# Stacked queries and keys brought in by groups of four pairs, each group with a semaphore of its own

## The reference

```
x = x + attention_a(layernorm(x))    # 16 heads, causal; queries and keys through low-rank products
x = x + ffn(layernorm(x))            # token shift, sigmoid gate, squared relu
x = x + attention_b(layernorm(x))    # 16 heads of 8, causal, queries and keys of length 1, scores times 8
x = x + ffn(layernorm(x))
```

## Time and profile before

| | before |
|---|---|
| three runs | 1116.02, 1116.97, 1117.32 us (median 1116.97) |
| profiled execution | 1122.54 us, of which the span of the profile is 1120.8 us |
| PE busy | 959.6 us, 86% of the span |
| DVE busy | 878.2 us, 78% |
| ACT busy | 769.6 us, 69% |
| POOL busy | 281.6 us, 25% |
| the queue of SP's transfers | 110.55 MB, 41.5% of 16 DMA engines' span |
| a batch in the steady part | 61 us (an output is stored at 523.40, 584.25, 645.10 us) |

### The profile page before, as it was taken

How to read it: one execution, slowest core, us unless ns; L and a number is a source line. 1 busy time by engine, 2 the same in 40 slices (tenths; PEclk the granted TensorE clock), 3 DMA queues, 4 the chain that set the end, 5 groups by cost and what they waited for, 6 DMA issues and landing times.

```text
span 1120.8 us, 36161 instructions
## 1 busy us (share of the span) xinstructions
PE 959.6 (86%) x15409; PEld 524.1 (47%) x15409; DVE 878.2 (78%) x2112; ACT 769.6 (69%) x1042; POOL 281.6 (25%) x264
## 2 busy tenths in 40 slices
PE   3668777979898989999999999899989999899694
PEld 1324344445454545555544545455544545455353
DVE  3757885779788898998989898989898898765632
ACT  2137464757677778777777888777877778688671
POOL 6011212212213123232323232222323232222212
PEclk8569898989998999999999999999999999899897
DMA  6155235425815427181817254362819062505130
GB/s 137 39 106 116 69 68 114 101 61 119 183 27 135 114 72 178 48 193 40 195 35 187 53 150 99 95 155 68 182 39 202 19 178 53 121 7 124 59 66 19
DMA packets 86145, 112.86 MB, mean 101 GB/s; under 512 B 13152, under 2 KB 79840, under 8 KB 79840
## 3 DMA queue, kind: packets, MB, share of 16 engines
q1 hardware_dynamic: 85984, 110.55, 41.5%
HBM read 55.22 MB, written 54.53 MB: 98 GB/s over the span
## 4 chain that ended last, share of the span: by engine, by line
PE 46%; DVE 30%; ACT 12%; issue 7%; DMA 2%; POOL 1%; SPq 0%; POOLq 0%; DVEq 0%; ACTq 0%
PE acc L722 16%; DVE rowmax L1074 12%; ACT prob L923 8%; PE pool L705 7%; PE pool L636 4%; PE pool L749 3%; PE pool L755 3%; DVE xn L1032 2%; PE pool L777 2%; PE pool L601 2%; PE pool L652 2%; DVE stats L1020 2%; PE pool L763 2%; PE pool L674 2%; DVE rest_k L1045 2%
## 5 line engine op out<-in xcount | busy, mean ns | idle before, releaser
L923 ACT ACTIVATE prob<-pool 128x1024 f32<-128x1024 f32 x576 | 565.5, 1029 | 150.5 <-PE pool L652 146.1
L1074 DVE TENSOR_REDUCE rowmax<-pool 128x2 f32<-128x1024 f32 (+7 forms) x480 | 357.8, 792 | 92.9 <-PE pool L652 89.9
L722 PE MATMUL acc<-prob,vals_a 128*32 128x512 f32 (+7 forms) x2048 | 169.3, 426 | 0.2 <-ACT prob L923 0.2
L722 PE MATMUL acc<-prob,vals_b 128*32 128x512 f32 (+7 forms) x2048 | 166.4, 426 | 1.2 <-DVE turned_b L1109 0.7
L636 PE MATMUL pool<-stack_ka,stack_qa 48*64 48x512 bf16 (+7 forms) x2048 | 118.7, 305 | 47.3 <-issue 13.9
L705 PE MATMUL pool<-stack_qa,stack_ka 51*64 51x512 bf16 (+7 forms) x2048 | 113.7, 302 | 31.3 <-DVE rowmax L1074 18.2
L705 PE MATMUL pool<-stack_qb,stack_kb 48*64 48x512 bf16 (+7 forms) x2048 | 113.7, 298 | 23.4 <-ACT prob L923 9.7
L652 PE MATMUL pool<-mask_t,ident_b 64*64 64x128 bf16 (+1 forms) x2304 | 130.7, 216 | 1.8 <-issue 1.8
L636 PEld LDWEIGHTS pool<-stack_ka,stack_qa 48*64 48x64 bf16 x2048 | 42.8, 109 | 141.0 <-ACT prob L923 59.3
L1284 POOL TENSOR_TENSOR rstd<-mv,minus_half 128x4 f32<-128x4 f32 x64 | 65.4, 1021 | 153.1 <-DVE mv L1027 153.1
L1296 POOL TENSOR_TENSOR parts_q<-rest_q,parts_q 128x512 bf16<-128x512 f32 x32 | 37.1, 1158 | 186.7 <-DVE parts_q L1048 186.6
(11 more groups left out here) (129 smaller groups left out, 1386.6 us busy)
## 6 DMA issues: line engine op xcount, KB each, us to landing
stack_qa<-scratch_qa SPq DMA_DIRECT2D x32, 384.0 KB, 7.9
stack_ka<-scratch_ka SPq DMA_DIRECT2D x32, 384.0 KB, 7.8
stack_kb<-scratch_kb SPq DMA_DIRECT2D x32, 384.0 KB, 5.6
stack_qb<-scratch_qb SPq DMA_DIRECT2D x32, 384.0 KB, 6.9
scratch_qa<-parts_q SPq DMA_DIRECT2D x16, 384.0 KB, 3.6
scratch_ka<-parts_k SPq DMA_DIRECT2D x16, 384.0 KB, 6.2
scratch_qb<-parts_q SPq DMA_DIRECT2D x16, 384.0 KB, 2.6
scratch_kb<-parts_k SPq DMA_DIRECT2D x16, 384.0 KB, 2.6
```

What stands on the lines that cost most here:

```text
L722: last = eng.matmul(acc[32 * j:32 * j + 32, BLK * blk:T], vals[a][:, blk, GROUP * g + j, :], prob[n % NPROB][:, k, at:at + T - BLK * blk], ...
L923: eng.activation(prob[n % NPROB][:, :, :], place["unit", n][0][:, :, :], ACT.Exp, scale=scale).then_inc(S["exped"], 1)
L1074: last = eng.tensor_reduce(to, of, axis=AX.X, op=ALU.max)
```

## The change

`restack` now takes a group instead of a tensor. In its first slot it brings group 0 of both tensors, and in its second slot group 1 of both; the order of the tensors in a slot is q, k for attention a and k, q for attention b. Each of its transfers is half as large (48 rows of 2048 elements in place of 4096), and there are twice as many: 256 instead of 128 in the whole program. Each group of each stack has a semaphore of its own. `row_maxima` and `attend` wait for their own group's alone, and SP waits, ahead of a group, only until that group's former contents are scored. The writes to scratch wait for both groups of the batch before.

```diff
-            for what in ("projected_", "part0_", "rest_", "part1_", "part2_", "written_", "stacked_"):
+            for what in ("stacked_" + n + str(g) for g in range(GROUPS)):
+                S[what] = ctx.enter_context(nc.semaphore("s_" + what))
+            for what in ("projected_", "part0_", "rest_", "part1_", "part2_", "written_"):
...
-            for k, n in enumerate("qk"):
-                yield e.restack(b, n, "a"), [max(at("restack_a")[k], front[-1] + 1, end_a[2] + k)]
+            for k in range(GROUPS):
+                yield e.restack(b, k, "a"), [max(at("restack_a")[k], front[-1] + 1, end_a[2] + k)]
...
-            for k, n in enumerate("kq"):
-                yield e.restack(b, n, "b"), [max(at("restack_b")[k], back[-1] + 1, of_b - 2 * SLOTS + k)]
+            for k in range(GROUPS):
+                yield e.restack(b, k, "b"), [max(at("restack_b")[k], back[-1] + 1, of_b - 2 * SLOTS + k)]
...
             def row_maxima(self, b, g, units):
                 eng, q = self.eng, self.q
-                q.wait_ge(S["stacked_qa"], 32 * (b + 1))
-                q.wait_ge(S["stacked_ka"], 32 * (b + 1))
+                q.wait_ge(S[f"stacked_qa{g}"], 32 * (b + 1))
+                q.wait_ge(S[f"stacked_ka{g}"], 32 * (b + 1))
...
-                        q.wait_ge(S[f"stacked_q{a}"], 32 * (b + 1))
-                        q.wait_ge(S[f"stacked_k{a}"], 32 * (b + 1))
+                        q.wait_ge(S[f"stacked_q{a}{g}"], 32 * (b + 1))
+                        q.wait_ge(S[f"stacked_k{a}{g}"], 32 * (b + 1))
...
-                    q.wait_ge(S[f"stacked_{n}{a}"], 32 * b)
+
+                    for g in range(GROUPS):
+                        q.wait_ge(S[f"stacked_{n}{a}{g}"], 32 * b)
...
-            def restack(self, b, n, a):
-                eng, q = self.eng, self.q
-                to = stack[n + a][b % len(stack[n + a])]
-                if n + a == "ka":
-                    q.wait_ge(S["ones_rows"], min(2 * b + 2, 4))
-
-                b_ = b - len(stack[n + a])
-                if b_ >= 0:
-                    q.wait_ge(S["scored"], unit_of[a, b_][-1] + 1)
-                q.wait_ge(S[f"written_{n}{a}"], 48 * (b + 1))
-                for r in range(2):
-                    src = scratch[n + a].rearrange("t (d r a) c -> (t d) r (a c)", d=D, r=2)[:, r, :]
-                    eng.dma_start(to[BLK * r:BLK * r + ROWS, :, :].rearrange("p a c -> p (a c)"),
-                                  src).then_inc(S[f"stacked_{n}{a}"], 16)
+            def restack(self, b, g, a):
+                eng, q = self.eng, self.q
+
+                for n in "qk" if a == "a" else "kq":
+                    to = stack[n + a][b % len(stack[n + a])]
+                    if n + a == "ka":
+                        q.wait_ge(S["ones_rows"], min(2 * b + 2, 4))
+
+                    b_ = b - len(stack[n + a])
+                    if b_ >= 0:
+                        q.wait_ge(S["scored"], unit_of[a, b_][9 * g + 8] + 1)
+                    q.wait_ge(S[f"written_{n}{a}"], 48 * (b + 1))
+                    for r in range(2):
+                        src = scratch[n + a].rearrange("t (d r a) c -> (t d) r a c", d=D, r=2)
+                        eng.dma_start(to[BLK * r:BLK * r + ROWS, GROUP * g:GROUP * g + GROUP, :],
+                                      src[:, r, GROUP * g:GROUP * g + GROUP, :]).then_inc(S[f"stacked_{n}{a}{g}"], 16)
```

## The result

| | before | after |
|---|---|---|
| median (runs of one chip) | 1116.49 us (1113.40 to 1117.32) | 1098.00 us (1094.58 to 1098.68) |
| ratio | | 0.9833, interval 0.9805 to 0.9862 |
| profiled execution, span | 1122.54 us, 1120.8 us | 1098.68 us, 1096.9 us |

The change makes the kernel 18.5 us faster. A second set of runs on another chip gave 1097.69 us beside 1116.0 (0.9843, 0.9812 to 0.9873).

The account below looks back on a forecast made before the run. PE and DVE were taken to alternate, with PE waiting for stacks only in batches 0 and 1; 4.9 + 4.8 + 1.0 = 10.7 us off the 1116.97 us median gave 1106.3 us, range 1104 to 1110 (8 in 10: 1103.5 to 1113).

Parts of the forecast that it names:

- These two, 18.9 us: PE's waits at the row maxima of batches 0 and 1, 13.9 and 5.0 us, claimed as its only stack waits.
- (a): Start, batch 0: group 0's stacks land earlier, PE starts at 26.8 instead of 31.75; gain 4.9 us.
- (b): Batch 1's stack wait: group 0 lands at 67.5 instead of 72.37, with the whole core standing; gain 4.8 us.
- (c): Behind batch 1's wait: PE's clock stays up without the idle 5 us; gain 1.0 us, at most 1.8.
- (d): 128 more SP issues, tightest in the repeating piece: six end 2.5 us before `max_rows` needs SP; cost 0.
- (e): DMA line: a 192 KB half takes half a whole transfer's time, 1.23 us; with a fixed share, 1.46 us.
- the half gain: Rival: a fixed share of 1.2 us per transfer leaves 2.5 us gain per place; about 1112 us, chance 0.12.
- no gain: Rival: the line mixes its transfers or the ramp waits again further on; about 1116 to 1118 us, chance 0.07.
- The slower rival: Rival: SP's issues delay `max_rows` in the repeating piece; 1134 us at 1.61 us an issue, chance 0.10.
- The 0.03: Chance left for a larger gain than summed, by the clock in other places.

Follow-up runs that it names:

- Run 4: Kernel before, with stacks by groups only for attention b of batch 0; 1110.19 us, ratio 0.9956.
- run 3: Kernel before, with stacks by groups only for attention a of batches 0 and 1; 1105.11 us, ratio 0.9909.
- third profile of before: Kernel before, unchanged, profiled again later to look for gaps of PE; 1117.10 us, span 1115.3 us.
- Run 1: Changed kernel's halved transfers and group semaphores, but each restack slot brings one whole tensor as before; 1105.36 us beside 1116.38, ratio 0.9911.
- run 7: Kernel before, with 80 overwritten matmuls put ahead of PE's wait for batch 1's stack; 1118.49 us beside 1120.09, ratio 1.0012.
- Run 11: Changed kernel, each transfer cut in two again by pairs, rows of 2 KB; 1121.24 us beside 1116.0, ratio 1.0023 to the kernel before.
- run 2: Changed kernel, but row maxima and scores wait for both groups of their stack; 1111.57 us, ratio 0.9958 to the kernel before.
- run 10: Kernel before, each stack transfer cut in two by partition rows, 24 rows of 8 KB; 1117.01 us beside 1116.0, ratio 1.0018.

## Why the prediction fell short

**The step that failed** is the sentence "These two, 18.9 us, are all that PE waits for stacks in the whole program". I took the list of who waited for line 1453 as complete. The third wait, of 4.3 us, is in the list of PE's waits as "L705 <- issue", in the same form as the 13.9 us that I had rightly read as a wait for a transfer, and in the chain as 4.29 us of "issue". I had looked at both views for 80 us only. Run 4 gives the place 6.2 us; run 3 leaves it out, is what I had argued, and gives 11.3. The prediction also had no term for the gaps inside units, 1.3 to 4.1 us in a profile.

**(a), batch 0, 4.9 us:** 5.05 by the third profile of before. Right, and PE's start (26.49) is within 0.3 us of the 26.8 foretold. Run 1 shows that a part of it is speed and not order.

**(b), batch 1, 4.8 us:** 5.4 by the third profile, 5.7 and 5.4 by the first and second. The wait itself was 5.55 us in the third (4.4 to 5.6 in the three), and all of it went.

**(c), the clock behind it, 1.0 us, at most 1.8:** 2.4. The mechanism is in the windows, of the same 128 matmuls in the kernel before and, with the stretch ahead of them, after:

```profile
72.50:81.30 8.80, 7.96 (x128) 3.70 (x132) 7.04 (x10) 2.05 (x2) 0.00 (x0) 0.53 0.01 2
```

```profile
56.50:61.40 4.90, 4.90 (x65) 1.75 (x61) 1.90 (x12) 3.54 (x5) 1.01 (x1) 0.60 0.96 207
61.40:68.20 6.80, 4.98 (x128) 2.58 (x124) 6.12 (x9) 3.02 (x4) 0.00 (x0) 1.00 0.41 78
```

They take 8.80 us at a clock of 0.53 and 6.80 at 1.00; from the first one's start to the last one's end it is 9.1 to 9.7 us in the three profiles of before and 7.2 after. My bound of 1.8 us took DVE's 6.43 us as work that has to be done in the stretch; with a fast PE the same matmuls end with one row maximum fewer done (9 instead of 10), so DVE's share shrinks too. The sentence that the prediction cites from the Trainium skill, TensorE: Matmul & The Clock Gate, "What's actually happening", is borne out where the gap is gone; in run 7, where the gap was filled, the clock fell all the same to 0.60 from 76 to 80 us, when PE took turns with DVE.

**(d), the issues at no cost:** right. SP is 2.0 us ahead of `max_rows` against 2.5 foretold, since an issue took 0.64 us and not 0.39, and the outputs keep their 61 us. Run 11 puts the edge between six issues and twelve.

**(e), a half takes half the time:** 1.23 us for a half was nearly right, 1.0 us in the mean, and I took that end for the wrong reason: the bytes move somewhat faster in halves, the opposite sign of a fixed share. The fit of the Trainium skill, DMA: Bandwidth & Descriptors, "Anatomy of one DMA", is given there for transfers issued by GpSimd, which I did not say; by it batch 0 would have gained 1.8 us. The trace of these transfers, issued by SP and queued, has 5.05 and disagrees.

**The rivals.** Neither the half gain nor no gain came about: halves land 1.0 us apart in the mean and 1.45 at the most, and a line that mixed its transfers would leave no difference between run 2 and the changed kernel, which are 13.6 us apart. The slower rival is a real mechanism (run 11), but it needed 0.8 us an issue for `max_rows` to be late, and the change's six took 0.64. The 0.03 that I left for a larger gain "by the clock in other places" named one of three causes. Of the missing 7.8 us the table has 3.5 in the third wait, 1.4 in the clock of (c), 0.8 in the longer waits of (a) and (b), and 2.0 in what follows, clock and gaps.

## What to carry to other kernels

Before saying that an engine waits for something only here, list all its waits over the whole program, those named "issue" too, and for each long one look which transfer landed just then: a wait for two semaphores can lose its name. A wait of PE in a ramp costs its length and can cost work at half clock behind it, here 2 to 3 us, so look at both; but filling such a wait with other matmuls did not make this kernel faster. When transfers are split so that the first consumer can start, stop where the issuing queue still has slack at its next deadline: halves gained 18.5 us and quarters gave all of it back. And look at gaps of an engine that nothing holds: code comes through the same DMA engines as data.

## What the runs showed of the hardware

- Queued halves of 4 KB rows moved the same bytes a little faster than whole transfers of 8 KB rows: a packet of 4 KB took 0.294 us in the mean and one of 8 KB 0.684, and with every half waited for the kernel was 0.4% faster (run 2). Halves of 24 rows of 8 KB had about 12 packets under way instead of 16 (DMA share 0.81 against 1.00 to 1.08), and brought nothing in the time (run 10). The prediction's bounds had allowed only the opposite sign.
- Where whole transfers with rows of 8 KB load the DMA engines, PE stood 1.1 to 2.7 us once or twice in an execution in the middle of a unit, and went on 1.2 to 1.6 us behind the end of a 16 KB packet of the instructions' queue (13 gaps in nine profiles); with rows of 4 KB or less no gap reached 1 us (seven profiles).
- The granted clock in the 12 us ahead of batch 0's first scores was 0.50 in one profile of the kernel before and 1.00 in two others, with PE idle in all of them, and the start of PE was the same to 0.4 us.
